# The key stacks of an attention pair issued from GpSimd's queue, not from SyncE's

## What is computed

```python
q, k, v = jnp.einsum('bsx,xMnd->Mbnsd', x, qkv)
a = jnp.einsum('bnsd,bntd->bnst', q, k) * 64 ** (-0.5)
cum = jnp.cumsum(rpe_bias[:, :s], axis=-1)                  # span of 256
bias = jnp.where(rel >= 0, cum[:, jnp.clip(rel, 0)], -30000.0)
mix = jnp.einsum('bnst,bntd->bnsd', jax.nn.softmax(a + bias), v)
x = layernorm(x + jnp.einsum('bnsd,ndx->bsx', mix, out_w))
xr = mu_r * x + (1 - mu_r) * x_prev;  xk = mu_k * x + (1 - mu_k) * x_prev
out = layernorm(x + sigmoid(xr @ W_r) * (square(relu(xk @ W_k)) @ W_v))
```

## Time and profile before

| | us |
|---|---|
| median of three runs | 1170.82 |
| the profiled execution | 1172.94 |
| its span | 1171.2 |
| TensorE matmul busy | 1110.0 |
| TensorE weight load busy | 793.0 |
| VectorE busy | 808.0 |
| ScalarE busy | 730.2 |
| GpSimd busy | 6.4 |

### The profile page before, as it was taken

The page is one execution under the profiler, slowest core; times in us unless marked ns, Lnnn a source line. Parts: engine busy times, 40 slices in busy tenths (PEclk is TensorE's granted clock), DMA queues, the critical chain, the costliest instruction groups (busy, mean ns, idle before and its releaser), DMA issues.

```text
span 1171.2 us, 21563 instructions
## 1 busy us (share of the span) xinstructions
PE 1110.0 (95%) x6973; PEld 793.0 (68%) x6973; DVE 808.0 (69%) x2121; ACT 730.2 (62%) x1857; POOL 6.4 (1%) x15
## 2 busy tenths in 40 slices
PE   6899999999999999999999999999999999999994
PEld 4666666667666677766677766677767677767673
DVE  2666666667676677876677776677777677776756
ACT  2666666667656567656666656567656566656633
POOL 1000000000000000000000000000000000000000
PEclk8999999999999999999999999999999999999997
DMA  7865566566655657656657665658655657665710
GB/s 191 226 148 144 143 142 159 142 176 165 156 138 143 159 152 187 156 142 164 155 154 185 158 149 135 157 152 205 156 149 140 154 152 187 157 152 137 231 54 20
DMA packets 113005, 180.71 MB, mean 154 GB/s; under 512 B 13152, under 2 KB 69360, under 8 KB 112896
## 3 DMA queue, kind: packets, MB, share of 16 engines
q1 hardware_dynamic: 110736, 178.42, 60.7%
q10 hardware_dynamic: 2160, 0.92, 0.3%
HBM read 58.41 MB, written 20.22 MB: 67 GB/s over the span
## 4 chain that ended last, share of the span: by engine, by line
PE 56%; SPq 17%; DMA 11%; DVE 8%; issue 5%; ACT 2%; DVEq 0%; POOL 0%; ACTq 0%
PE ps_o L1015 18%; SPq L300 14%; PE ps_rows L974 12%; DMA mix_tile<-mix_transposed 9%; PE ps_t L991 8%; PE ps_m L949 7%; PE ps_m L1031 4%; DVE prob L657 3%; SPq L361 2%; PE ps_m L954 2%; DVE mix_sb L688 2%; DMA prob<-in_L_attn_x 1%; PE ps_rows L1087 1%; PE ps_o L991 1%; DVE k_lo L643 1%
## 5 line engine op out<-in xcount | busy, mean ns | idle before, releaser
L498 ACT ACTIVATE prob<-prob,low 128x128 f32<-128x128 f32 (+7 forms) x512 | 394.7, 772 | 111.3 <-DVE low L657 105.2
L657 DVE CUSTOM_DVE_ANT_0 prob<-ps_rows,table 128x128 f32<-128x128 f32 (+7 forms) x512 | 379.8, 750 | 47.4 <-PE ps_rows L974 32.2
L974 PE MATMUL ps_rows<-stacks 128*128 128x512 f32 (+3 forms) x1536 | 401.2, 372 | 5.1 <-issue 2.9
L991 PE MATMUL ps_t<-ident,prob 128*128 128x128 f32 x1984 | 310.6, 277 | 6.5 <-ACT pt L516 3.6
L991 PEld LDWEIGHTS ps_t<-ident,prob 128*128 128x128 f32 x1984 | 230.3, 140 | 90.0 <-issue 73.6
L681 DVE COPY pt<-ps_t 128x256 f32<-128x256 f32 (+2 forms) x320 | 178.2, 565 | 147.5 <-PE ps_t L991 147.1
L1015 PE MATMUL ps_o<-pt,v_pair 128*64 128x512 f32 (+3 forms) x1536 | 268.7, 492 | 0.0
L974 PEld LDWEIGHTS ps_rows<-stacks 128*128 128x128 f32 x1536 | 246.1, 191 | 25.8 <-issue 3.1
L1015 PEld LDWEIGHTS ps_o<-pt,v_pair 128*64 128x64 f32 x1536 | 101.9, 137 | 176.1 <-issue 163.9
L516 ACT ACTIVATE pt<-ps_t 128x512 f32<-128x512 f32 (+3 forms) x352 | 162.7, 462 | 90.2 <-PE ps_t L991 89.9
L949 PE MATMUL ps_m<-x_cur,w_cur 128*128 128x512 f32 x250 | 130.9, 605 | 2.2 <-issue 1.3
(11 more groups left out here) (118 smaller groups left out, 637.9 us busy)
## 6 DMA issues: line engine op xcount, KB each, us to landing
stacks<-k_hi SPq DMA_DIRECT2D x126, 256.0 KB, 4.4
stacks<-k_lo SPq DMA_DIRECT2D x126, 256.0 KB, 4.9
inv_all<-inverse_sums SPq DMA_DIRECT2D x128, 128.0 KB, 3.3
stacks<-q_hi SPq DMA_DIRECT2D x63, 256.0 KB, 3.9
stacks<-q_lo SPq DMA_DIRECT2D x63, 256.0 KB, 4.2
mix_transposed<-mix_sb SPq DMA_DIRECT2D x62, 256.0 KB, 4.0
table<-bias_by_distance SPq DMA_DIRECT2D x64, 192.0 KB, 3.7
mix_tile<-mix_transposed SPq DMA_DIRECT2D x24, 512.0 KB, 5.4
```

The costliest lines, as they stand in the source:

```text
L498: nc.scalar.activation(row, row, ACT.Exp, bias=low[:, r:r + 1], scale=-1.0, accum_out=total[:, r:r + 1]).then_inc(s_exp, 1)
L657: nc.vector.tensor_tensor_reduce(prob[:, r % PSLOTS, 0:width], ps_rows[:, score_at(r):score_at(r) + width], table[n % 2][:, h, 0:width][:, ...
L974: ins = nc.tensor.matmul(ps_rows[:, at + c0:at + c1], q_st(h, n)[:, P * i:P * i + P], k_st(h, n, low_part)[:, c0:c1], start=(low_part == 0 ...
L991: ins = nc.tensor.transpose(t_bank[TBANK[k]][:, P * b:P * b + P], prob[:, r % PSLOTS, at:at + P], ident[:, :])
```

## The change

The eight key stacks of a pair leave SyncE's `step` and are issued by GpSimd, on its own DMA queue, in a loop over the pairs. They raise semaphores of their own, one for each head (`s_stack_k`), and the two engines that waited for all stacks, ScalarE before it overwrites `q_hi` and TensorE before the first row of a group of four, now wait for both semaphores. GpSimd waits for the low part of the keys (`s_lo`), and, for the set of stacks to be free, for the scores of pair n-1 (`s_score`). The stacks of pair 0 stay on SyncE.

```diff
@@ SyncE's step @@
                 spread_inverse(n, 0)
-                if more:
-                    sp.wait_ge(s_lo, 4 * n + 8)
-                    for h in range(2):
-                        stack_k(n + 1, h, s_stack[h])
                 if n + 1 >= TILE_LAG:
                     tile_loads(n + 1 - TILE_LAG)
@@ GpSimd, behind its memsets @@
+            for n in range(PAIR_STEPS - 1):
+                pool.wait_ge(s_lo, 4 * n + 8)
+                if n > 0:
+                    pool.wait_ge(s_score, NROWS * n)
+                for h in range(2):
+                    for low_part, part in enumerate((k_hi, k_lo)):
+                        for rows in (slice(0, D), slice(D, P)):
+                            pool.dma_start(k_st(h, n + 1, low_part)[rows, :].bitcast(F32),
+                                           part[D * h:D * h + D, :].bitcast(F32)).then_inc(s_stack_k[h], 16)
@@ ScalarE, before q_hi is written @@
-                        act.wait_ge(s_stack[h], 96 * m)
+                        act.wait_ge(s_stack[h], 32 * m + 64)
+                        if m > 1:
+                            act.wait_ge(s_stack_k[h], 64 * (m - 1))
@@ TensorE, before a score row @@
-                    pe.wait_ge(s_stack[h], 96 * n + 96)
+                    pe.wait_ge(s_stack[h], 32 * n + 96)
+                    if n > 0:
+                        pe.wait_ge(s_stack_k[h], 64 * n)
```

More of the change, by code:

```diff
@@ L206, in build @@
         s_stack = [sem(f"stacked{h}") for h in range(2)]
+        s_stack_k = [sem(f"keys_stacked{h}") for h in range(2)]
         s_table = [[sem(f"table{a}{h}") for h in range(2)] for a in range(2)]
```

## The result

The changed kernel took 1213.3 us in the median of four runs (1199.5 to 1221.0), beside 1170.9 for the kernel before, 3.6% more. Two of the four, 1217.7 and the profiled 1221.0, lie over 1.5% above the fastest and count as slow runs; without them the ratio is 1.028, interval 1.018 to 1.037. A second set of four runs (1211.8 to 1223.2), beside twelve of the kernel before, gave 1216.0 against 1175.0, ratio 1.037 (1.030 to 1.044). So it is slower by 3 to 4%, with a spread of 21 us in the first set where the kernel before has 8. The forecast was slower, 1186, range 1153 to 1218. The profiled execution of the changed kernel is its slowest of the first set, 1221.0 us; another one, of 1214.8 us from the second set, is read beside it, and shows the same stalls.

The account below looks back on a forecast made before the run. TensorE, 95% busy, was taken as the bound. From the profiled 1172.94 us, 34.5 us of new stalls (23 x 1.5) less 19.3 us of removed waits gave 1188.1, or 1186 us for the median; range 1153 to 1218.

Parts of the forecast that it names:

- the forecast case itself: Tile steps: TensorE stalls 0.9 to 2.2 us each at slot 12, giving 1172 to 1202 us; chance 0.45.
- a slow GpSimd: Rival: at 2.0 us an issue, GpSimd's pace delays the fourth stack, stalling 2.7 us in all 31 steps; 1235 us, chance 0.15.
- What it removes: TensorE's waits: all 18.2 us for `mix_tile` and 1.1 us in step 0 go, together 19.3 us.
- Step 0's 1.06 us: TensorE's loss in step 0 while SyncE sat for the inverse sums; claimed to go, as GpSimd doesn't wait for them.
- The slack of 1.2 us: Head 0's fourth key stack lands at 594.8 and is needed at slot 12, at 596.02, before the change.
- No second stall: Slot 0: head 1's last stack lands at 602.3, before its need, moved by 1.5 us to 603.1.
- D: TensorE's stall in a tile step, taken as 1.5 us in 23 steps; time is 1151.5 + 23 D, level at 0.84.
- `mix_tile`'s work ahead of the fourth stack: DMA engines: the tile's loads, 1.7 to 2.45 us of work, taken as 2.2, all go in before head 0's fourth stack.
- The issue by GpSimd: GpSimd's queue: 1.2 us an issue assumed, counted as 0.5 us of delay to head 0's fourth stack.
- The stacks are still in time: Rival at slot 12: the DMA engines have room, D is 0 to 0.3, time 1151.5 to 1158 us; chance 0.25.
- the two cancel: Rival: D between 0.3 and 0.9, with 1.7 us of tile work and GpSimd as quick as SyncE; 1163 us, chance 0.13.
- Something else holds `mix_tile`: Rival: `mix_tile` stays held, such as by SyncE's wait for the mix in DRAM; 1171 us, chance 0.02.

Follow-up runs that it names:

- The held tile: Changed kernel, with SyncE waiting for head 0's four key stacks to land before issuing the tile's loads: 1176.9 us, ratio 1.005.
- the small tile: Changed kernel, with `mix_tile`'s load cut to one of eight pairs for every tile but the first (output not the layer's): 1151.4 us, ratio 0.981.

## Why the prediction was right, and where it was off

The time came out inside the stated range, 5 us under its upper end, and outside the 1172 to 1202 of the forecast case itself: the loss was 42 us where the forecast has 15. The direction and the place of the stall were forecast; that the range held was in part luck, as its upper part had been taken in for a slow GpSimd, which is not what came.

**What it removes: right.** `mix_tile`'s 18.2 us of waits went entirely. It was issued at 379.54, 0.6 us after the keys were ready at 378.97, for 1.2 us foreseen, and landed 8.1 us after them in the mean, 595.8 on the forecast's scale of 594 to 598. Step 0's 1.06 us shrank to 0.2.

**The sign and the mechanism: right.** The stall is at slot 12, for head 0's stacks, in the tile steps and not in steps 1 to 7, because the tile's load shares full DMA engines with them. The held tile and the small tile show it from two sides. The slack of 1.2 us, from which the loss was reckoned, was as read: 10.7 - 7.3 = 3.4 us of delay less 1.2 gives the 2.2 us of stall. "No second stall" at slot 0 held in 21 of the 23 tile steps.

**The size of D: off.** I took D = 1.5 us; at slot 12 it was 49.9 / 23 = 2.17 (2.37 in the second profile). The term that was mis-sized is the first, `mix_tile`'s work ahead of the fourth stack. I put it at 2.2 us and said that nothing more could be lost; head 0's last stack came 10.7 - 7.8 = 2.9 us later in tile steps than in steps without a tile (10.9 - 7.6 = 3.3 in the second profile), above even the 2.45 of my upper bound. The total was right: head 1's last stack, behind all of the work, came 2.8 us later than before (12.1 to 14.9), for 2.7 forecast. What was wrong is the order. The sum let the work pass in single file. In the step shown, the fourth stack landed after head 1's first though it was issued before it. So it did in 9 of the 23 tile steps (10 in the second profile), where it landed 11.7 us after the keys in the mean; in the other 14 it was 10.0, near the 9.8 of the forecast. In the kernel before it happened in none of them, and in the changed kernel in none of steps 1 to 7. With 4 KB rows in place of 512-byte pieces it was 6 steps. When the tile's load starts matters too: in the two steps with a stall at slot 0 it was issued 1.6 and 2.2 us after the keys were ready, for 0.6 in the others; head 0's last stack then landed early, at 8.9 and 9.1 us, and head 1's late, at 15.6 and 16.7. Why one copy overtakes another in one step and not in the next the traces don't show, and it stays open. 23 x 0.67 = 15 us of the miss are here, and 3 us in the two stalls at slot 0.

**The issue by GpSimd: the term was right, its working was not.** An issue took GpSimd 0.52 us in the median, less than SyncE's median of 0.60, where I had taken 1.2:

```profile
L452 POOL DMA_DIRECT2D stacks<-k_hi x124: 509/517/705, 46.3 to 1129.5; - x124
```

Even so head 0's last stack lands 7.8 us after the keys are ready in steps 1 to 7, against 7.3 before (7.6 and 7.3 by the second profile): the 0.5 us that I had taken, by another way. GpSimd starts 0.3 us after the keys where SyncE needs 0.03; the rest has no cause that the traces show. The rival in which GpSimd is slow to issue (chance 0.15, 1235 us) had the wrong cause and is out. The Trainium skill (DMA: Bandwidth & Descriptors, Latency and other measured facts) has 1 us to the first byte against 0.6 us, as cited in the prediction. The trace doesn't bear a later start out: in the step without a tile at 80 us the first stack itself landed 3.1 us after its issue, for 3.3 from SyncE.

**The clock: missing.** I priced a stall at its length. TensorE's matmuls took 16.6 us longer in all, with 13 stretches at the lower level, and the runs spread because it is not the same number of stretches each time. The profile with 8 of them (59 us at the lower level in the whole span, for 76) has 8.5 us more than before and took 1214.8 us. That is the second part of the miss. Together: 1188.1 forecast for a profiled execution, + 15.4 for slot 12, + 3.0 for slot 0, + 16.6 for the clock are 1223.1 against 1221.0 measured. For the second profile, 1188.1 + 20.1 + 8.5 are 1216.7 against 1214.8.

**The rivals.** "The stacks are still in time" was open by 1.2 us of slack and is ruled out by the waits, and "the two cancel" as well. "Something else holds `mix_tile`" is out: it went at once. The room in the DMA engines that I had counted for the first rival was used by moving work forward: they were 1.06 busy from 383 to 391 us, and 0.08 from 395 on. VectorE did not slow down beside GpSimd's issues: with the small tile it is busy 808.5 us with them and 807.9 without.

## What to carry to other kernels

A second queue doesn't make room on DMA engines that are already full. Before moving a transfer forward or to another queue, find what it will run beside, and read the slack of that: here 1.2 us of slack stood against 3.4 us of delay. The same transfer moved into a stretch with room gained 1.9% (1.4 to 2.3), on the old queue. A total of work on the DMA engines tells when the last of several transfers lands, here within 0.1 us; it did not bound the delay of one in the middle. And price a stall of TensorE of two to four microseconds above its length: the clock afterwards cost 8.5 and 16.6 us here beside stalls of 55 and 53 us.

## What was not expected of the hardware

- GpSimd's issue of a 64 x 4 KB copy from SBUF to SBUF took 0.52 us, hardly varying (509 to 519 ns for the 124 low parts), where SyncE's of the same copy took 0.48 to 2.33 us: GpSimd had issued all eight 4.3 us after the keys were ready, in 16 of 23 tile steps before the first had landed, and was not held back.
- Two DMAs issued in order on GpSimd's queue landed out of order, 391.4 for the fourth and 390.5 for the fifth, in 9 of 23 tile steps.
- Six idle-time matmuls a step, 1.5 us of useless work in 23 steps, made the kernel 12 us faster in the median, with a granted clock of 1.00 for 0.97 over the middle.
- In step 16 GpSimd's first issue came 3.3 us after the keys were ready, for 0.3 in the other steps, in both profiles of the changed kernel. With the held and the small tile TensorE stood 1.8 and 2.0 us in that one step. The cause is not shown.
